# First stage of a decoder layer: projections by halves of the heads, query and key halves kept in chip memory, values by ScalarE and GpSimd, maximum pieces in pairs

## What is computed

```python
q = (x @ wq + bq).reshape(B, S, H, Dh).transpose(0, 2, 1, 3)      # k, v alike
scores = jnp.einsum('bhqd,bhkd->bhqk', q, k) / jnp.sqrt(jnp.float32(Dh))
scores = jnp.where(causal[None, None], scores, jnp.float32(-jnp.inf))
out = jnp.einsum('bhqk,bhkd->bhqd', jax.nn.softmax(scores, axis=-1), v)
...
t_act = jax.nn.gelu(jnp.matmul(text_features, learnable_matrix), approximate=False)
weight_map = jnp.einsum('bqc,bkc->bqk', query, t_act)
out = jnp.einsum('bqk,bkc->bqc', weight_map, text_features)
```

## Time and profile before

| | |
|---|---|
| median of 3 runs | 885.47 us (881.0 to 888.93) |
| profiled execution | 883.31 us, of which the trace's span 881.6 us |
| VectorE, ScalarE, GpSimd busy in the span | 66%, 60%, 32% |
| TensorE busy in the span | 94% |
| mean granted TensorE clock | 0.972 of full |
| first stage, to attend's first matmul | 111.26 us |

### The profile page before, as it was taken

How to read it: one execution, slowest core, us unless ns; L and a number is a source line. 1 busy time by engine, 2 the same in 40 slices (tenths; PEclk the granted TensorE clock), 3 DMA queues, 4 the chain that set the end, 5 groups by cost and what they waited for, 6 DMA issues and landing times. The chain is left out here.

```text
span 881.6 us, 19681 instructions
## 1 busy us (share of the span) xinstructions
PE 826.9 (94%) x7444; PEld 500.5 (57%) x7445; DVE 578.2 (66%) x1070; ACT 528.2 (60%) x781; POOL 286.3 (32%) x191
## 2 busy tenths in 40 slices
PE   5789899999999999999999797999999999999994
PEld 2344433333333333333332486889999999877883
DVE  4746678999999999999991286873333333332466
ACT  4401077787777778877788575644444444433555
POOL 5000069334444444334632000022333333311133
PEclk9979879999999999999999997999999999999997
DMA  7792024443343334444332399011111111100142
GB/s 212 235 251 54 1 108 145 145 145 125 109 128 111 131 131 135 145 144 145 109 110 108 134 420 399 3 37 31 50 48 50 51 49 48 48 20 25 61 148 98
DMA packets 40746, 102.42 MB, mean 116 GB/s; under 512 B 7773, under 2 KB 25374, under 8 KB 36318
## 3 DMA queue, kind: packets, MB, share of 16 engines
q1 hardware_dynamic: 35966, 90.73, 30.7%
q0 software_dynamic: 4000, 10.36, 3.7%
q10 hardware_dynamic: 704, 0.27, 0.1%
HBM read 68.69 MB, written 32.37 MB: 115 GB/s over the span
## 5 line engine op out<-in xcount | busy, mean ns | idle before, releaser
L168 DVE TENSOR_REDUCE partial<-ring 128x1 f32<-128x512 f32 (+3 forms) x509 | 308.8, 669 | 31.2 <-PE ring L150 22.2
L656 ACT ACTIVATE probs<-scores 128x1024 f32<-128x1024 f32 (+1 forms) x320 | 271.0, 904 | 63.3 <-PE scores L703 32.4
L719 PE MATMUL acc<-probs,values 128*32 128x512 f32 (+3 forms) x1280 | 170.1, 541 | 0.9 <-ACT acc_sb L661 0.7
L1303 PE MATMUL turned<-mats,weights 128*128 128x256 f16 (+1 forms) x1488 | 160.7, 263 | 2.4 <-DVE mats L1551 1.5
L1327 PE MATMUL ops<-weights,work 128*128 (+1 forms) x1320 | 151.2, 275 | 6.3 <-DVE res L1577 5.1
L1146 ACT ACTIVATE hid<-turned 128x512 f32<-128x512 f32 (+1 forms) x112 | 65.7, 586 | 145.8 <-PE turned L1303 132.7
L631 POOL TENSOR_TENSOR a_w_in<-a_w_in,w_scale 128x2304 f32<-128x2304 f32 x16 | 64.4, 4028 | 271.0 <-DMA a_w_in<-w_all 271.0
L1303 PEld LDWEIGHTS turned<-mats,weights 128*128 (+1 forms) x1488 | 136.7, 98 | 23.0 <-issue 4.1
L150 PE MATMUL ring<-kstack,qstack 48*128 48x512 f16 (+1 forms) x580 | 145.1, 352 | 2.2
L1327 PEld LDWEIGHTS ops<-weights,work 128*128 128x128 f16 x1320 | 129.4, 99 | 24.0 <-DVE res L1577 5.4
L1559 DVE TENSOR_TENSOR work<-hid,work 128x512 f16<-128x512 f32 (+1 forms) x112 | 76.1, 683 | 100.7 <-ACT work L1151 100.7
(11 more groups left out here) (196 smaller groups left out, 787.0 us busy)
## 6 DMA issues: line engine op xcount, KB each, us to landing
a_w_in<-w_all SPq DMA_DIRECT2D x16, 1152.0 KB, 7.9
w_split_d<-a_w_out SPq DMA_DIRECT2D x16, 1152.0 KB, 5.6
weights<-w_split_d SPq DMA_DIRECT2D x9, 2048.0 KB, 26.5
qstack<-q_split SPq DMA_DIRECT2D x96, 64.0 KB, 2.8
kstack<-k_split SPq DMA_DIRECT2D x96, 64.0 KB, 2.8
attn<-by_token SPq DMA_DIRECT2D x16, 256.0 KB, 4.0
xT_sb<-xT SPq DMA_DIRECT2D x4, 512.0 KB, 9.8
q_split<-qk SPq DMA_DIRECT2D x16, 128.0 KB, 2.7
```

Of the source, the lines that this page charges most:

```text
L168: return nc.vector.tensor_reduce(out=found[:, places[0]:places[-1] + 1:step], in_=bank[:, 0:WIDTH[n]].rearrange("p (k w) -> p k w", k=len( ...
L656: nc.scalar.activation(probs[:, s % 2, at:at + w], scores[half][:, first:first + w], ACT.Exp).then_inc(exp_done, 1)
L719: mm = nc.tensor.matmul(acc[VW * j:VW * (j + 1), QB - w:QB], values[:, h, k0 + j], probs[:, s % 2, at:at + w], start=first, stop=last)
L1303: mm = nc.tensor.matmul(hps[b][:, j * TW + first_row:j * TW + first_row + w], weights[:, a, bass.ds(at + (k * HID + (b * HB + j) * P), P)] ...
```

## The change

- **Half of the heads first.** The 16 groups now run over c (half of the columns, so heads 0 to 7, then 8 to 15), in it over the quarters, in each query and key. The three products come in the order high x high, low weights x high x, high weights x low x, each with its own wait. Three PSUM banks instead of two.
- **Halves kept on chip.** `qk16` now holds all halves. ScalarE writes the high half from PSUM with the bias, VectorE the low half from PSUM in one instruction. The scale 1/4 goes into the exponential, into the copy of the maximum and (as 4) into the row of ones. Stacks 0 to 3 are copied from `qk16`; the keys of stack 0 are issued by ScalarE. The store to `q_split` and `k_split` (for heads 4 and up) comes behind these loads. The loads of small tensors and context all go on SP's queue ahead of them.
- **Values.** ScalarE copies them out of PSUM, GpSimd adds the bias in chip memory.
- **Pieces.** They have three banks of their own and are formed by twos, behind places given by `pieces_behind`. The last context product is copied by ScalarE.
- `xT_sb` and `t_act` share memory with `attn` and `x_split`.

```diff
+def load_first_stack(queue, stack, qk16, what, h, signal):
+    for group in range(2):
+        for s in range(SLOTS):
+            at = group * GROUP + s * DH
+            queue.dma_start(stack[at:at + DH, h, :], qk16[h * DH:(h + 1) * DH, 0, what, (Q_HALF, K_HALF)[what][s], :]).then_inc(signal, 16)
+def pieces_behind(kind, n):
+    if kind == "m":
+        return 2 if n % 4 == 3 else 1 if n == DC * CT - 1 else 0
+    return 2 * {"qk": n >= NQ * 4 - 2, "v": n % 2, "t": n % 3 != 2}[kind]
...
 # SP
-            for q in range(NQ):
-                for n in range(4):
-                    sp.wait_ge(qk_lo, 4 * q + n + 1)
-                    what, c = n // 2, n % 2
-                    for half in range(2):
-                        sp.dma_start((q_split, k_split)[what][half, c * P:(c + 1) * P, q * QB:(q + 1) * QB],
-                                     qk16[:, n, half, :]).then_inc(qk_stored[n], 16)
...
+            sp.wait_ge(qk_lo, NG0)
+            load_first_stack(sp, qstack, qk16, 0, 0, stack_in[0])
+            for what, stack in enumerate((qstack, kstack)):
+                load_first_stack(sp, stack, qk16, what, 1, stack_in[1])
             sp.dma_start(res[:], x.rearrange("(t p) d -> p t d", p=P)).then_inc(res_in, 16)
+            for h in range(2, NSTACK):
+                for what, stack in enumerate((qstack, kstack)):
+                    load_first_stack(sp, stack, qk16, what, h, stack_in[h])
+            sp.wait_ge(qk_lo, NG)
+            for c in range(DC):
+                for what, split in enumerate((q_split, k_split)):
+                    sp.dma_start(split[:, c * P:(c + 1) * P, :].rearrange("a p n -> p a n"), qk16[:, c, what]).then_inc(qk_stored, 16)
...
 # ScalarE
+            for g in range(NG):
+                c, q, what = group_of(g)
+                if c == 0 and what == 0 and q + 1 < NQ:
+                    first_half_x(q + 1)
+                act.wait_ge(qk_ready, g + 1)
+                nc.scalar.activation(qk16[:, c, what, 0, q * QB:(q + 1) * QB], qk_ps[g % 3][:], ACT.Identity,
+                                     bias=b_cols[:, what, c:c + 1]).then_inc(qk_hi, 1)
+                if g == NG0 + 1:
+                    act.wait_ge(qk_lo, NG0)
+                    load_first_stack(nc.scalar, kstack, qk16, 1, 0, stack_in[0])
...
+            for t in range(NT):
+                act.wait_ge(v_ready, t + 1)
+                nc.scalar.activation(values[:, :, t, 0:DH], vt_ps[t % 2][:, 0:D].rearrange("p (h d) -> p h d", d=DH),
+                                     ACT.Copy).then_inc(v_copied, 1)
...
 # GpSimd
+            for t in range(NT):
+                pool.wait_ge(v_copied, t + 1)
+                nc.gpsimd.tensor_tensor(values[:, :, t, 0:DH], values[:, :, t, 0:DH], bv_rows[:].rearrange("p (h d) -> p h d", d=DH),
+                                        ALU.add).then_inc(v_done, 1)
...
 # VectorE
+                nc.vector.scalar_tensor_tensor(out=qk16[:, c, what, 1, cols], in0=qk_ps[g % 3][:], scalar=b_cols[:, what, c:c + 1],
+                                               in1=qk16[:, c, what, 0, cols], op0=ALU.add, op1=ALU.subtract).then_inc(qk_lo, 1)
+                take_pieces(pieces_behind("qk", g))
...
 # TensorE
+                    if formed == 0:
+                        pe.wait_ge(pool_done, 6)
+                        pe.wait_ge(swapped, 16 * 2 * 2)
+                    if formed % NPIECE == 0:
+                        pe.wait_ge(stack_in[slot], STACK_DMAS)
+                    if formed >= NRING:
+                        pe.wait_ge(piece_done, formed - NRING + 1)
+                    form_piece(nc, piece_ps[formed % NRING], qstack, kstack, ident16, hide_keys, slot,
+                               FIRST_PIECES[formed], formed % 2).then_inc(piece_ready, 1)
+                    formed += 1
...
 # attend
-                                         ACT.Exp).then_inc(exp_done, 1)
+                                         ACT.Exp, scale=QK_SCALE).then_inc(exp_done, 1)
```

More of the change, by code:

```diff
@@ L340, in first_half_x @@
                 act.wait_ge(xT_in[q], 16)
-                nc.scalar.activation(x_split[:, 0, :, cols], xT_sb[:, :, cols], ACT.Copy).then_inc(hi_done, 1)
+                nc.scalar.activation(x_split[:, 0, :, cols], xT_sb[:, :, cols], ACT.Copy).then_inc(x_hi, 1)
             first_half_x(0)
[L344 to L349, removed]
+            act.wait_ge(qk_bias_in, 16)
@@ L360, in _ @@
[L360 to L362 removed]
+                    act.wait_ge(small_in, 16 * 3)
+                    nc.scalar.activation(w_split[:, 2, 0], w_in[:, 2], ACT.Copy).then_inc(vo_hi, 1)
+                    nc.scalar.activation(wo_split[:, 0], w_in[:, 3], ACT.Copy).then_inc(vo_hi, 1)
@@ L426, in _ @@
+            dve.wait_ge(qk_w_hi, 1)
+            nc.vector.tensor_tensor(w_split[:, 0:2, 1], w_in[:, 0:2], w_split[:, 0:2, 0], ALU.subtract).then_inc(qk_w_lo, 1)
             second_half_x(0)
-            for g in range(4 * NQ):
-                if g % 4 == 1 and g // 4 + 1 < NQ:
-                    second_half_x(g // 4 + 1)
+            for g in range(NG):
+                c, q, what = group_of(g)
+                if c == 0 and what == 1 and q + 1 < NQ:
+                    second_half_x(q + 1)
@@ L466, in _ @@
+            assert taken == len(FIRST_PIECES)
         @block.tensor
         def _(pe):
[L468 to L477 removed]
+            formed = 0
@@ new lines, in form_pieces @@
+            def form_pieces(count):
+                nonlocal formed
+                for _ in range(count):
+                    slot = formed // NPIECE
+                    if formed == 0:
[8 more added lines that the diff above has]
+                    formed += 1
+                    if formed == NPIECE + 2:
+                        pe.wait_ge(first_max_found, 1)
+                        nc.tensor.transpose(qk_ps[1][0:NT, 0:P], neg_max[:], ident32[:]).then_inc(first_max_turned, 1)
@@ new lines, in _ @@
+            for g in range(NG):
+                c, q, what = group_of(g)
+                if g == 0:
+                    pe.wait_ge(qk_w_hi, 1)
+                pe.wait_ge(x_hi, q + 1)
+                if g >= 3:
+                    pe.wait_ge(qk_lo, g - 2)
+                n = 0
+                for a, b in ((0, 0), (1, 0), (0, 1)):
+                    if g == 0 and a == 1:
+                        pe.wait_ge(qk_w_lo, 1)
+                    if b == 1:
+                        pe.wait_ge(x_lo, q + 1)
+                    for k in range(DC):
+                        mm = nc.tensor.matmul(qk_ps[g % 3][:], w_split[:, what, a, k, c * P:(c + 1) * P],
```

216 lines of the change are left out of this document (92 added, 124 removed).

## The result

| | before | after |
|---|---|---|
| median | 883.24 us (879.33 to 888.93, 4 runs) | 859.54 us (858.83 to 859.96, 4 runs) |
| ratio, 95% interval | | 0.9726 [0.9667, 0.9785] |
| profiled span | 881.6 us | 858.1 us |
| attend's first matmul | 111.26 us | 89.12 us |
| from there to the end of the span | 770.3 us | 769.0 us |

The account below looks back on a forecast made before the run. The first stage's chain through TensorE was the bound. Values from 34.0, then 46.8, 1.65, 1.0 and 0.5 put attend at 84.0 instead of 111.3; 27.3 off the 885.47 median gave 858 us, range 851 to 870.

Parts of the forecast that it names:

- my first sign of being right: Attend's first matmul was to come at 84 us (80 to 88).
- another of my signs: No clock under 0.9 between 30 and 80 us.
- Start at 9.0: The first group's first matmuls need only the high half of x, so TensorE starts at 9.0 us.
- Projections, 1.29 a group: Sixteen projection groups of six matmuls take 20.6 us, plus waits of 0.4 and 1.85 for low halves of x.
- ScalarE stands 2.7 us, TensorE waits 1.0: In the projections, six copy issues at 0.45 us hold ScalarE 2.7 us; group 13's bank costs TensorE 1.0 us.
- The port rule of the Trainium skill: First stack's copies read 16 partitions, four ports, estimated 109 GB/s: stack whole near 32.5, wait 1 to 2 us.
- Stack whole at 31: First stack full at about 31 us, wanted at 31.7; margin of 0.7 thin, so 1.0 us of wait summed.
- Pairs at 0.57: Two pieces cost one insertion, 0.52 us, 0.57 with masks; values, t_prime and context product sum to 46.8 us.
- Rival C: Pairs don't overlap between full-height matmuls, or each mask breaks the pair: 12 us back, 870 us; chance 0.08.
- The end: Behind the last context matmul: piece 0.4, reduce 0.8, then 0.44 to attend's first matmul; 1.65 us in the sum.
- rival E: Slower: first stage waits for stores behind 48 copies, if these run below 50 GB/s; 900 us at 40; chance 0.03.
- Rival B: First stack late and the clock falls: 3 us more wait and 5 of clock, 866 us; chance 0.2.

Follow-up runs that it names:

- repeated kernel: The changed kernel run once more with nothing altered, as reference for the experiments: 859.29 us, ratio 0.9732.
- other rows: The changed kernel with the three blocks of a stack read from three different heads' partitions (scores wrong): 856.33 us, ratio 0.9694.
- late pieces: The kernel with keys on SP, with no pieces in the projections; first pair behind the second value tile, four pieces moved behind the context product: 855.64 us.
- keys on SP: The changed kernel with stack 0's six key copies issued by SP behind the query copies, none by ScalarE: 857.88 us, ratio 0.9714.
- early low halves: The kernel with late pieces, VectorE making the next quarter's low half of x before the first group's low half, not the second's: 853.09 us, repeated 852.28.
- the warming: Eight 128x512 matmuls with unread result before TensorE's first group, added to the kernel with late pieces and early low halves: 852.09 us.

## Why the prediction came out as it did

The forecast was 858 us in 851 to 870; measured were 859.54. The direction, the mechanism and the three main gains are as predicted. The hit within 2 us is partly luck. The sum said 27.3 us, and the profiled span fell by 23.5, 3.8 less. Of this error 2.2 did not show, because I took the saving off a median that was 2.2 above the profiled execution. Attend's start, my first sign of being right, came at 89.12, outside the 80 to 88 that I gave it, and the clock fell between 30 and 80, against another of my signs.

By the steps of the prediction:

- **Start at 9.0.** Measured 10.03. The high half is made when x has landed, and it began at 8.83 instead of 7.89. The repeated kernel had 7.08 and a first matmul at 8.28, and all profiles of changed kernels lie between 8.28 and 10.47, so this moves from run to run.
- **The clock row.** I read four slices below nine tenths; there are five, the third, fifth, sixth, 25th and last. The three that bear on the first stage are read rightly.
- **Projections, 1.29 a group, with a wait of 0.4 and three more of 1.85 in all for low halves.** Three waits of 0.54 to 0.57 came. With the 0.18 of modelled end that each hides they cost 2.2, for the 1.85 of the sum. The step that failed is that I priced all matmuls at 0.215: the first ones follow each other in 0.43, which cost 1.3; the wait of 0.4 that I had there did not come. Groups 0 to 12 took 20.3 us instead of 19.1.
- **ScalarE stands 2.7 us, TensorE waits 1.0.** This is the term that was mis-sized most. The price of an issue, 0.45, came from the earlier trace rows, a load of 2 KB from HBM. It was 0.885, the wait 3.14, and the clock fell behind it, which made the 5.0 us of groups 13 to 15 and two pairs 6.5. Together 3.7 us of the 6.2 by which the values start late (40.2 against 34.0). The experiment with other rows shows the cause, the late pieces show the price, 3.65. The port rule of the Trainium skill that I weighed was right about the rate (104 GB/s measured), but I let it act on the landing only, not on the engine that issues.
- **Stack whole at 31, wait of 1.0 in the sum.** The last key copy was only issued at 30.94, and copies took 4.5 us to land, yet the wait didn't show, since the bank's wait stood ahead of it. With the keys on SP it showed, 2.20 us.
- **Pairs at 0.57, 46.8 us for values, t_prime and context.** 47.6 measured: 14.36 for 15.6, 17.70 for 16.3, 15.54 for 14.9. Between value tiles a pair costs 1.74 - 1.38 = 0.36. Of the nine insertions in t_prime two cost 1.1 instead of 0.57: the one at 66.9, whose pieces are made of several blocks of 128 and 256 columns, each with its mask, and the one at 71.3, which waits for a reduce and has the turning of the maximum in it. Rival C is refuted, pairs are worth 11.35 us.
- **Values.** ScalarE 0.384 as priced, GpSimd 0.723, inside the bounds of 0.42 and 1.22, done well before 60. It was right to cost it at nothing, and VectorE's relief is worth 1.8 us, not the whole 6.7 that it loses in work.
- **The end.** 1.3 us from the last context product to attend, for 1.65. SP's queue was slower than I had it, stores issued at 60.6 to 64 and the maximum row at 72.66 instead of 66, still hidden: rival E had its room of 15 us.
- **Attend.** 0 for a clock that stays up, bound 2.9. It gained 1.3, and the profiles span 2.4.
- **Rival B** (a wait of 3 us and a fallen clock) happened in its form, 3.14 us and 0.50 up to 36.6, but at the bank instead of the stack. It ended at 859.5 and not at 866: the half clock lasted 3.4 us and cost 1.5, not the 5 of that rival.

The parts as the experiments price them: pairs 11.35 us; beside late pieces, the half of the heads first 7.9 and the copies in the chip 7.35 (both feed the same wait, so they don't add up); values 1.8. Against the repeated kernel after, late pieces and early low halves bring another 6.2 to 7.0, to 853.09 in one measurement and 852.28 in the other; the warming adds nothing that can be told.

## What to carry to other kernels

An issue of a transfer is work on the engine that issues it, and its price is that of the transfer's own kind: take it from a row with the same source and size, and ask what the engine's other consumers wait for meanwhile. Matmuls of few rows that are slipped between full-height ones cost by the insertion and not by the piece (0.39 us for one as for two), so gather them by row group. Place them behind the landing of what they read, with room, since the waits of 2.9 us and more in these projections also cost clock.

## What was not expected of the hardware

- 64 KB copies inside the chip were issued every 0.63 us from one queue whatever they read, against 0.46 from HBM. Two queues reading the same 16 partitions got 104 GB/s together, reading three sets of them 177.
- The first matmuls run at half speed while the clock row says 1.00: the 128x512 ones follow each other in 0.43 us until 12.9 in the kernel after, until 13.6 in the repeated one with early low halves, and until 12.5 to 15.4 over all profiles of changed kernels without the warming. Eight matmuls ahead of them, themselves 0.43 apart, brought 0.215 from the second matmul on. In each trace the first entry of the clock record lies where this spacing ends (12.7, 13.6 and, with the warming, 9.1 us), so a 1.00 ahead of it is the lack of an entry; there the spacing of matmuls tells the clock.
- A TensorE wait of 3.14 us at the end of the projections went with half clock for 3.4 us, one of 8.56 us with half clock from inside the wait on, 10.3 us in all, waits of 1.67 and 2.20 us there with none, and a stop of 1.2 at attend's start with anything between none and 6.8.
